# Two-layer graph network and expert mixture on one core: the first mixture sorted in two token halves, its first half gathered back during the second half's experts

## The reference, cut to what matters

```python
# block 2: x + _L0_ffn_ref(_layernorm(x), Wg, bg, W1, b1, W2, b2)
gate_logits = xf @ Wg + bg
top_w, top_i = jax.lax.top_k(gate_logits, 2)
top_w = jax.nn.softmax(top_w, axis=-1)
w_dense = jnp.sum(jax.nn.one_hot(top_i, E) * top_w[..., None], axis=1)
for e in range(E):                       # E = 8, W1[e] 128x512, W2[e] 512x128
    h = jax.nn.gelu(xf @ W1[e] + b1[e], approximate=False)
    out = out + w_dense[:, e:e + 1] * (h @ W2[e] + b2[e])
# block 3, its start: x + _L1_gnn_ref(_layernorm(x), adj, ...)
h = jax.nn.relu(jnp.einsum('ts,bsh->bth', adj, x @ Wg0 + bg0))
h = jax.nn.relu(jnp.einsum('ts,bsh->bth', adj, h @ Wg1 + bg1))
# then LSTM windows of 1 to 4 nodes over h
```

## Time and profile before

| What | Value |
|---|---|
| Median of 3 runs (lowest to highest) | 1780.99 us (1779.0 to 1786.6) |
| Span of the profiled execution, first to last instruction | 1732.9 us |
| PE / DVE / ACT / POOL busy, share of the span | 72% / 48% / 43% / 34% |
| Mean granted TensorE clock, share of 2.4 GHz | 0.860 |
| First `route` / `experts` / `gnn1`, start to end | 443 to 509.5 / 509.5 to 792 / 792 to 1011 us |
| DMA | 68.34 MB, mean 39 GB/s |

### The profile page before, as it was taken

How to read it: one execution, slowest core, us unless ns; L and a number is a source line. 1 busy time by engine, 2 the same in 40 slices (tenths; PEclk the granted TensorE clock), 3 DMA queues, 4 the chain that set the end, 5 groups by cost and what they waited for, 6 DMA issues and landing times. The chain is left out here.

```text
span 1732.9 us, 27194 instructions
## 1 busy us (share of the span) xinstructions
PE 1239.7 (72%) x5977; PEld 878.7 (51%) x5978; DVE 839.6 (48%) x3397; ACT 752.5 (43%) x1922; POOL 596.0 (34%) x1079
## 2 busy tenths in 40 slices
PE   2444327389379999994887889998984995899800
PEld 1233216369268999993443433444332453799800
DVE  5777999675862222224667623333337236311122
ACT  3555436112275455542454445444445553654400
POOL 4666237000015656555777200000000000355376
PEclk9999756695699999996888899999996996699955
DMA  9200000003002222231111000000000110022233
GB/s 265 68 1 1 1 0 2 0 1 97 0 6 67 68 72 69 70 67 49 50 49 44 18 0 0 0 0 0 0 0 7 42 42 6 23 69 67 60 95 99
DMA packets 86126, 68.34 MB, mean 39 GB/s; under 512 B 11014, under 2 KB 76108, under 8 KB 86060
## 3 DMA queue, kind: packets, MB, share of 16 engines
q1 hardware_dynamic: 73068, 41.01, 8.3%
q0 software_dynamic: 12992, 26.63, 6.4%
HBM read 40.99 MB, written 26.61 MB: 39 GB/s over the span
## 5 line engine op out<-in xcount | busy, mean ns | idle before, releaser
L1250 POOL COPY g_idx<-sitter 128x1 int32 (+1 forms) x72 | 11.0, 179 | 543.3 <-POOLq L1112 526.7
L1667 PE MATMUL ps<-BIG,w_ihT 128*128 x364 | 162.2, 589 | 20.6 <-ACT e_go L1689 15.0
L1310 ACT ACTIVATE c_H<-ps,c_b 128x256 f32<-128x256 f32 x284 | 117.3, 470 | 131.9 <-PE ps L1339 131.0
L1254 POOL DMA_INDIRECT c_Z<-z,c_idx x142 | 138.3, 974 | 81.0 <-POOLq L1252 57.5
L1452 POOL DMA_INDIRECT d_Y<-y,seat x128 | 130.2, 1017 | 61.4 <-issue 36.9
L1354 PE MATMUL ps<-w_dn,c_H 128*128 x1136 | 139.2, 276 | 1.8 <-ACT c_H L1310 1.6
L1339 PE MATMUL ps<-c_ZT,c_w 128*128 128x256 f32 x568 | 136.3, 383 | 1.4 <-ACT c_ZT L1298 1.4
L1354 PEld LDWEIGHTS ps<-w_dn,c_H 128*128 128x128 f32 x1136 | 132.5, 192 | 3.8 <-issue 3.4
L1667 PEld LDWEIGHTS ps<-BIG,w_ihT 128*128 128x128 f32 x364 | 69.3, 194 | 108.5 <-issue 108.5
L1673 PE MATMUL ps<-e_hs,w_hhT 128*128 128x512 f32 (+1 forms) x256 | 110.8, 575 | 12.8 <-DVE e_hs L1719 12.8
L1339 PEld LDWEIGHTS ps<-c_ZT,c_w 128*128 128x128 f32 x568 | 103.6, 193 | 13.4 <-ACT c_ZT L1298 2.1
(11 more groups left out here) (495 smaller groups left out, 2896.8 us busy)
## 6 DMA issues: line engine op xcount, KB each, us to landing
y<-c_ys SPq DMA_DIRECT2D x71, 128.0 KB, 1.8
z<-ZB SPq DMA_DIRECT2D x32, 256.0 KB, 2.2
y<-g_ys SPq DMA_DIRECT2D x36, 128.0 KB, 1.8
out_dram<-X SPq DMA_DIRECT2D x32, 128.0 KB, 1.9
c_Z<-z,c_idx POOLq DMA_INDIRECT x142, 2.6
w_up<-in_L_ffn_W_dram SPq DMA_DIRECT2D x1, 2048.0 KB
w_dn<-in_L_ffn_W_dram SPq DMA_DIRECT2D x8, 256.0 KB
w_dn<-in_L_ffn_Wd_dram SPq DMA_DIRECT2D x8, 256.0 KB
```

The lines of the kernel that those rows point to most:

```text
L1250: pool.tensor_copy(idx[h][u][:, :], k.sitter[:, ds(t * HALVES + h, 1)]).then_inc(copied, 1)
L1254: pool.indirect_dma_start(Z[u][:, h, :], None, z, bass.IndirectOffsetOnAxis(ap=idx[h][u][:, 0:1], axis=0)).then_inc(fetched[u], 16)
L1310: act.activation(H[u][:, c, :], UP[u][c // 2][:, c % 2 * SLOT_TILE:(c % 2 + 1) * SLOT_TILE], ACT.Gelu, bias=(b1[u] if w_up is not None els ...
L1667: last = pe.matmul(o, k.w_ihT[:, w, :], state(i, u, s, p, wide, lanes), start=True, stop=(s == 0))
```

## The change

The first `route` becomes `route_shares`: the 64 token tiles are two halves of 32, and each half is sorted by itself into a region of 72 blocks of 128 slots. Each expert's share of a region is padded to 128 slots only. There are now 144 blocks, 72 tiles of 256 slots. A tile can hold two experts, one in each half of it.

The first `experts` becomes `experts_in`, written out instead of looped. SP loads the up weights of each half tile (128x512, 256 KB) from DRAM, three tiles of buffers; `w_up0` and its 2 MB load at the start are gone. PE does eight up matmuls of 128 columns and ACT eight Gelus of 128x128 per tile. POOL gathers `z0` rows into a ring of 64 blocks (in `BIG`), straight from `sitter`. After 112 of them it waits until the 36 tiles of the first half are stored, and then gathers the first half's result rows, two per token tile, with the remaining 32 `z0` blocks among them. DVE combines and takes statistics of one token tile per expert tile from tile 40 on.

`gnn1` starts with 32 token tiles combined: it scales eight groups at once, gathers the other 32 tiles only, and combines three of them per group from the third group on. ACT normalises two groups ahead, and its gates are split up and put among the other steps.

```diff
-SLOTS0 = (2 * B * N + E * (SLOT_TILE - 1)) // SLOT_TILE * SLOT_TILE
+SHARES = 2
+SHARE = TILES // SHARES
+REGION = -(-((2 * SHARE * P + E * (P - 1)) // P * P) // SLOT_TILE) * SLOT_TILE // P
+SLOTS0 = SHARES * REGION * P
+Z_RING, Z_SEMS = 64, 8
+Z_FIRST = 112
+Y_RING = 6
+LAG = 40
...
+def route_shares(nc, k, sem):
...
+            for h in range(SHARES):
+                with dve.Fori(0, TURNS) as i:
+                    for b in range(DEEP):
...
+                        dve.tensor_scalar(ohh[b][:, :], k.irow[:, h * REGION:(h + 1) * REGION], hi[c][:, ds(t, 1)],
+                                          k.token[:, ds(t, 1)], ALU.is_equal, ALU.mult).then_inc(oh_ready, 1)
...
+def experts_in(nc, k, sem, z, y, w_up):
...
+            for n in range(Z_FIRST):
+                fetch(n)
+            for u in range(2):
+                pool.wait_ge(stored[u], 16 * (FIRST // 2))
+            for m in range(SHARE):
+                if m >= Y_RING:
+                    pool.wait_ge(used, m + 1 - Y_RING)
+                for c in range(2):
+                    pool.indirect_dma_start(rows[m % Y_RING][c][:, :], None, y[0],
+                                            bass.IndirectOffsetOnAxis(ap=k.seat[c][:, m:m + 1], axis=0)
+                                            ).then_inc(y_in[m % Y_RING], 16)
+                if Z_FIRST + m < NT * HALVES:
+                    fetch(Z_FIRST + m)
...
+            def weights(t):
+                if t >= 3:
+                    sp.wait_ge(up, (t - 2) * PER)
+                for h in range(HALVES):
+                    e = sp.value_load(k.expert[0:1, t * HALVES + h:t * HALVES + h + 1], min_val=0, max_val=E - 1)
+                    sp.dma_start(w1[t % 3][h][:, :], w_up[ds(e, 1), :, :].rearrange("a d h -> (a d) h")).then_inc(w_in[t % 3], 16)
...
+            for t in range(NT):
+                if t + 2 < NT:
+                    weights(t + 2)
+                if t >= 1:
+                    store(t - 1)
...
+            biases(0)
+            for t in range(NT + 1):
+                if t + 1 < NT:
+                    biases(t + 1)
+                if t >= 1:
+                    bias_out(t - 1)
+                if 0 <= t - LAG < SHARE:
+                    combine(t - LAG)
+                if 0 <= t - LAG - 1 < SHARE:
+                    stats(t - LAG - 1)
...
+                    for h in range(HALVES):
+                        act.activation(H[u][:, c, h * P:(h + 1) * P],
+                                       UP[u][c // 2][:, c % 2 * SLOT_TILE + h * P:c % 2 * SLOT_TILE + (h + 1) * P],
+                                       ACT.Gelu, bias=b1[u][h][:, c:c + 1]).then_inc(gelu, 1)
...
+                            pe.matmul(UP[u][c // 2][:, c % 2 * SLOT_TILE + h * P:c % 2 * SLOT_TILE + (h + 1) * P],
+                                      w1[t % 3][h][:, c * P:(c + 1) * P], ZT[u][:, h * P:(h + 1) * P],
+                                      start=True, stop=True).then_inc(up, 1)
...
 def gnn1(nc, k, sem, y):
...
-            for n in range(TILES):
-                b = n % AHEAD
+            for m in range(TILES - SHARE):
+                b, n = m % AHEAD, SHARE + m
...
+            scale(0, early)
+            done, scaled_to = 0, early
             for g in range(GROUPS + 3):
-                for j in range(GT):
-                    if g < GROUPS:
-                        combine(g * GT + j)
-                        stats(g * GT + j)
+                for j in range(3):
+                    if g >= 2 and done < TILES - SHARE:
+                        combine(done)
+                        stats(done)
+                        done += 1
                     if j == 0 and g >= 3:
                         new_state(g - 3)
-                if g < GROUPS:
-                    scale(g)
                 if 1 <= g <= GROUPS:
                     add_bias(g - 1)
+                if scaled_to < GROUPS and done >= (scaled_to + 2 - early) * GT:
+                    scale(scaled_to, 2)
+                    scaled_to += 2
...
-        k.w_up0 = sb("w_up0", [P, E, HID])
-                (k.w_up0[:, :, :], up0),
...
-        route(nc, k, sem, "r", [k.K1, k.K2], SLOTS0, SLOT_TILE)
-        experts(nc, k, sem, "c", z0, y0, SLOTS0, None, k.w_up0, k.w_dn0, k.b_up0, k.b_dn0)
+        route_shares(nc, k, sem)
+        experts_in(nc, k, sem, z0, y0, f0_W1)
```

More of the change, by code:

```diff
@@ L1368, in _, with scale_of @@
             sp.wait_ge(stored[1], 16 * (NT // 2))
+def scale_of(dve, link, k, r, bits, half, root):
+    tt_, ts_, stt = dve.tensor_tensor, dve.tensor_scalar, dve.scalar_tensor_tensor
+    a, b, m = k.va[:, r], k.vb[:, r], k.mean[:, r]
+    me, ve, mo, vo = (k.st6[:, r, n] for n in (1, 2, 4, 5))
+    link.need(link.n)
+    got_even = link.put(tt_(a, me, mo, ALU.subtract))
+    got_both = link.put(tt_(b, ve, vo, ALU.add))
+    link.put(tt_(m, me, mo, ALU.add))
+    link.need(got_both)
+    got_sum = link.put(ts_(b, b, 1.0 / D, EPS, ALU.mult, ALU.add))
+    link.need(got_even)
+    link(tt_(a, a, a, ALU.mult))
+    link.need(got_sum)
+    link(stt(out=a, in0=a, scalar=0.25, in1=b, op0=ALU.mult, op1=ALU.add))
+    inverse_root(dve, link, k, a, k.rstd[:, r], bits, half, root)
+    return stt(out=k.mean[:, r], in0=m, scalar=-0.5, in1=k.rstd[:, r], op0=ALU.mult, op1=ALU.mult)
@@ L1441, in gnn1 @@
         gates = {0: gi, 2: gg, 3: go}
-        bits, half, root = (own.enter_context(nc.sbuf_tensor(f"d_{n}", [P, GT], F32)) for n in ("bits", "half", "root"))
+        bits, half, root = (own.enter_context(nc.sbuf_tensor(f"d_{n}", [P, SHARE], F32)) for n in ("bits", "half", "root"))
         block = own.enter_context(nc.Block())
@@ L1459, in _, with combine, stats, scale @@
             tt_, ts_, stt = dve.tensor_tensor, dve.tensor_scalar, dve.scalar_tensor_tensor
[L1461 to L1488, removed]
+            def combine(m):
+                b = m % AHEAD
+                dve.wait_ge(fetched[b], 32 * (m // AHEAD + 1))
+                combined(dve, link, k, SHARE + m, Y[b]).then_inc(used, 1)
+            def stats(m):
+                dve.wait_ge(used, m + 1)
+                link.put(dve.bn_stats(k.st6[:, SHARE + m, :], k.X[:, SHARE + m, :]))
+            def scale(first, groups):
+                t, w = first * GT, groups * GT
+                scale_of(dve, link, k, slice(t, t + w), bits[:, 0:w], half[:, 0:w], root[:, 0:w]).then_inc(scaled, groups)
             def add_bias(g):
@@ L1528, in _, with normalized @@
         def _(act):
-            def normalized(g):
+            def normalized(g, tiles):
                 u = g % 2
-                act.wait_ge(scaled, g + 1)
-                if g >= 2:
-                    act.wait_ge(mixed, g - 1)
-                for j in range(GT):
+                for j in tiles:
                     n = g * GT + j
@@ L1567, in _ @@
                     act.activation(HT[u][:, :], UP[:, :], ACT.Relu).then_inc(h_ready, 1)
-                if g < GROUPS - 1:
-                    normalized(g + 1)
-                if g >= 1:
-                    gate(g - 1)
-                    act.wait_ge(cell, g)
-                    act.activation(tcs[1 - u][:, :], cs[1 - u][:, :], ACT.Tanh).then_inc(tanh_c, 1)
+                if 1 <= g <= GROUPS:
+                    if g >= 3:
+                        act.wait_ge(hid, g - 2)
+                    gate(g - 1, 0)
+                if ahead:
+                    normalized(g + 2, range(2, 3))
+                if 1 <= g <= GROUPS:
+                    gate(g - 1, 1)
+                    gate(g - 1, 2)
+                if ahead:
+                    normalized(g + 2, range(3, 4))
         @block.tensor
```

295 lines of the change are left out of this document (273 added, 22 removed).

## The result

The changed kernel takes 1904.24 us (four runs, 1896.1 to 1907.35), the one before 1780.43 beside it: 1.0683 times as long, 95% interval 1.0658 to 1.0707. Forecast was 1733, with a chance of 0.08 for slower.

The account below looks back on a forecast made before the run. PE bounds the experts, the gather and steps to DVE bound gnn1, route nearly fills DVE, ACT and PE. 0 + 8.5 - 11.7 - 45 = -48.2 us, 1780.99 to 1733; own range 1715 to 1750, to 1766 with rivals 1, 3, 4.

Parts of the forecast that it names:

- Four of that width take 1.02 us in the second route instead of 1.15: First route's marker loop: 72 columns instead of 142 save 4.2 us over 32 times, offset by other costs to about 0.
- PE's sum: Experts: PE's matmul time per tile rises from 3.74 to 3.80 us with eight narrow up matmuls.
- ACT's low end: Experts: a narrow Gelu costs 0.26 us, making ACT's loop through PE 3.69 us, just under PE.
- rival 1: Experts: ACT becomes the bound, narrow Gelu 0.33 us, loop 4.25 us, +30 us, total 1763; chance 0.15.
- rival 2: Experts: weight loads at half rate, 158 GB/s, bind at 4.8 us a tile, +70 us, total 1803; chance 0.08.
- Rival 4: Experts: POOL falls behind at 1.70 us an issue, tiles starve for 26 us, total 1759; chance 0.08.
- Nothing, but those 10 us are all the margin there is: Experts, POOL: gathers add no time; POOL is done at 263 us, tile 71 is turned at about 276.
- Part 3, hand-over: Last expert bias add to gnn1's first mix: 9.1 us instead of 20.8, -11.7 us.
- PE's own work, 7.9 us, is the bound: gnn1's groups: PE's work sets the pace once gathers are halved; 8.6 us a group taken.
- six per group where there are any: 6 x 1.26 = 7.6 us: gnn1's groups: POOL's gather issues need 7.6 us a group, below PE's 7.9, eight tiles fetched ahead.
- Rival 3: gnn1: fixed orders of PE, ACT and DVE keep groups at 10.5 us, +27 us, total 1760; chance 0.14.
- with the 48.1 us around it, unchanged: Whole kernel: 48.1 us between profiled span 1732.9 and median 1780.99 lie around the span and stay.

Follow-up runs that it names:

- The wide markers: Changed kernel with the first route's marker matrices 144 columns wide again in both loops; 1878.9 us, one run.
- the rings of 64, 32 and 8: Changed kernel (ring of 64 z0 blocks, 1904.24 us) with the ring cut to 32 (1870.0 us) or to 8 (1837.43 us), remaining z0 gathers spread among y0 pairs.
- Without the early fetch: Changed kernel with no y0 gathers in the experts, all 128 in gnn1, z0 ring of 8, markers 144 wide; 1833.63 us.
- the second profile: The kernel before, unchanged, profiled once more; time 1778.66 us, span 1776.9 against 1732.9 in the first profile.
- two outstanding: Changed kernel where POOL waits before each z0 gather until the one two before has landed, and likewise between y0 pairs; 1845.29 us.

## Why the prediction was wrong

**Part 1, route: 0 forecast, +15.7 measured.** The step that failed is "Four of that width take 1.02 us in the second route instead of 1.15". I priced the narrower markers on DVE and left PE out. The loop fell to TensorE's lower level (granted clock 0.50, that is 1.2 GHz) and took 53.7 us from first to last marker instead of 43.0. The wide markers bring 10.0 back. Of the other 5.7 us, 4.4 lie ahead of the loop, where the doubled tables are, for which I had put 3; no run takes them apart.

**Part 2, experts: +8.5 forecast, +168.2 measured.** PE's sum (3.80) is right: 3.79 us where POOL is silent. ACT's low end is right: eight Gelus in 2.18 us are 0.27 each, so rival 1 falls; the loop through ACT did not become the bound. The rule of the Trainium skill ("ScalarE: Activation LUTs", What ACT_TABLE_LOAD costs) gave 0.29 and is close, but its effect, a loop of 3.97, did not come. The loads are hidden, so rival 2 falls. The Trainium skill's line on loads ("DMA: Bandwidth & Descriptors", Rules for kernel authors) is about the highest bandwidth, and 183 GB/s was enough here. Rival 4 falls as put: POOL kept 1.25 us an issue until its ring was full; it was the others that fell behind.

The step that failed is POOL's, "Nothing, but those 10 us are all the margin there is". I asked whether POOL would be done in time, and never what its gathers do to others. The long row at the start costs 77 us (95.2 against 18.1), shown by the rings of 64, 32 and 8. From tile 39 on, three tiles cost 20.6 us over 3.79 each and the next 25 some 2.1 us each, 52 us, all beside rows of `y0` and `z0` gathers; tiles 4 to 24 cost 0.27 each, 5.5. That is 155 us of the missing 160. Without the early fetch the tiles of the second half keep 4.09 us. My "32 rounds of three gathers take 121 us, beside 36 tiles of 137 us" describes a row almost without a pause.

**Part 3, hand-over: -11.7 forecast, -12.3 measured.** Right, by its own steps.

**Part 4, groups: -45 forecast, -29 measured** (152.0 us for the 15 steps). The six steps after the last gather take 7.7 us each (1133.60 - 1087.45 = 46.2), better than my 8.6; the nine with gathers 11.8 on the mean (1087.45 - 981.64 = 105.8). But these nine are of two kinds. Four take 7.5 to 7.8 us although POOL issues, so "PE's own work, 7.9 us, is the bound" holds there. The other five take 9.4, 23.6, 16.4, 9.9 and 16.2, 37 us over 7.7 each. In the longest ACT stands for 14.25 us of the row of 22 gathers; in the two of 16 us DVE stands for 5.94 and 3.85 us beside gathers, and the granted clock falls to 0.50 after it, so that matmuls of 2.84 us take up to 5.00. POOL's rate is not what holds them up, since POOL itself waits for DVE in five places, 31.5 us in all. So the step that failed is the one of Part 2 again: "six per group where there are any: 6 x 1.26 = 7.6 us" asks only whether POOL keeps up. That the miss is no larger than 16 us is in part luck: the ten other steps took 76.5 us where I had 86. Rival 3 came near in its size (10.1 on the mean) but not in its cause: the free groups show no loop of waits of 10.5 us.

**The sum.** "with the 48.1 us around it, unchanged" was wrong too: the time is 1.9 us over the span. The 44 us between the two profiles of before were crawl in `gnn1` and `combine1`. Against the second profile, which stands for the timed runs, the change gains 53 us from the first mix to `lstm` (221.3 to 168.3) and loses 4.6 behind it. The difference between span and median was the warning for Part 2, and I did not follow it.

No version with the early fetch that I tried beat the kernel before, nor did the one without it. That the sort by half and the narrow padding could pay with another pacing isn't excluded.

## What to carry to other kernels

Gathers issued on POOL aren't free for the engines beside them, even when the DMA engines are three quarters idle: count how many follow each other without a semaphore wait that really waits; beside a full PE two in a row cost 0.1 to 0.3 us here and three 1.8. A deep ring of gather buffers can be worse than a shallow one. Where a median stands well above the profiled span, find out what the profiled execution lacks before working from its durations; and price a narrower operation on every engine that takes part, the clock of TensorE included.

## What the runs showed of the hardware that I had not expected

- During an unbroken row of gathers on POOL (1.25 us apart) the other engines go on by an instruction in 0.70 or 1.4 us, or stand, until the row ends or up to 8 us longer (614.6 to 622.7 in the changed kernel). It set in about 20 us into the row at the start of the experts and of `gnn1`, and 6 us into the row of 18 gathers at 768.5. Short rows of three to six stop them for 1 to 5 us and let go 1 to 1.5 us after the row. Copies of POOL's own don't help; waits of 0.67 us on the mean (1.92 - 1.25, with two outstanding) do. Whether it is the breaks or the lower rate, and what sets the price of a row, stays open.
- It is no matter of DMA bandwidth (0.25 busy), of loads on SP's queue, of the loading of code (no packet on its queues in `combine1`'s crawl), or of the number of the others' instructions (40 fewer a tile gained nothing).
- The same code can run with the crawl and without it: `gnn1` and `combine1` of the kernel before did both. All runs here carry the profiler's recording; whether it has a part in this could not be tried, and what makes the engines stand stays open.
- The Trainium skill ("DMA: Bandwidth & Descriptors", SWDGE vs HWDGE vs iDMA) tells of DVE locking GpSimd out while GpSimd writes its descriptors, to which DMAs issued from SP are said to be immune. That is another effect; here SP's issues took 3.65 us instead of 1.44 in a row of gathers.
- A float32 matmul of 144 columns took 286 ns with the clock mostly at its upper level, one of 72 columns 421 ns with the clock at 0.50 over the whole loop.
